# A two-layer network on one core: in the first layer's loop a key projection a step later, queries ahead of the per-token output's transposes, two side products last in their steps, and no expert sums beside the softmax

## The reference, cut to what matters

```
x = x + tanh(g_xattn[0]) * attention0(layernorm(x), ctx)     # 16 heads of 64, causal
x = x + tanh(g_ffn[0])   * mix0(layernorm(x))
x = x + tanh(g_xattn[1]) * attention1(layernorm(x), ctx)     # second layer
x = x + tanh(g_ffn[1])   * ffn1(layernorm(x))

def mix0(x):                       # every token by itself
    h = rmsnorm(x) * gamma1
    q = h @ Wq + bq                                  # 16 heads of 16
    k, v = split((h @ Wdown + bdown) @ Wup + bup)    # through 64 features
    att = softmax_over_g(q_h . k_g / 4)              # 16 x 16 for each token
    out = att @ v
    x = x + (out @ Wo + bo)
    h2 = rmsnorm(x) * gamma2
    gate = softmax(h2 @ Wg + bg)                     # 8 experts
    return x + sum_e gate[e] * (h2 @ We[e])
```

## Time and profile before

| | |
|---|---|
| median of 3 runs | 2502.51 us (2501.88 to 2504.15) |
| the profiled execution, its own time | 2502.84 us |
| its span from the first to the last instruction | 2501.0 us |
| busy: PE, DVE, ACT, POOL | 89%, 59%, 51%, 41% of the span |
| mean granted clock of TensorE | 0.961 of full speed |

### The profile page before, as it was taken

How to read it: one execution, slowest core, us unless ns; L and a number is a source line. 1 busy time by engine, 2 the same in 40 slices (tenths; PEclk the granted TensorE clock), 3 DMA queues, 4 the chain that set the end, 5 groups by cost and what they waited for, 6 DMA issues and landing times.

```text
span 2501.0 us, 47888 instructions
## 1 busy us (share of the span) xinstructions
PE 2227.4 (89%) x16000; PEld 1887.5 (75%) x16000; DVE 1480.4 (59%) x3922; ACT 1267.7 (51%) x3969; POOL 1023.1 (41%) x907
## 2 busy tenths in 40 slices
PE   5888899898888888888875799999999999999998
PEld 4667677777777777777664688888888888888888
DVE  4466666767667676676767635555555555555551
ACT  5655655556555565555633434455544444445541
POOL 1255555565555655556446213333332322333320
PEclk9999999999999999999977799999999999999999
DMA  4000000000000000000110200000000000000000
GB/s 154 8 12 14 6 17 17 17 13 4 17 17 17 13 4 17 17 17 4 39 32 13 110 16 7 13 17 17 17 17 17 17 17 16 5 13 17 17 9 9
DMA packets 26000, 51.40 MB, mean 21 GB/s; under 512 B 6160, under 2 KB 7312, under 8 KB 24784
## 3 DMA queue, kind: packets, MB, share of 16 engines
q1 hardware_dynamic: 25936, 50.57, 6.0%
HBM read 42.17 MB, written 8.39 MB: 20 GB/s over the span
## 4 chain that ended last, share of the span: by engine, by line
PE 57%; DVE 15%; ACT 8%; POOL 6%; issue 6%; DVEq 4%; POOLq 2%; DMA 0%; ACTq 0%
PE l_ffn L1714 13%; POOL l_prod L385 5%; PE l_ffn L161 4%; PE l_attn L161 4%; PE l_ffn L162 4%; PE l_ffn L163 4%; PE l_attn L1675 4%; PE l_attn L163 3%; PE l_attn L162 3%; DVEq L735 3%; PE l_side L161 3%; PE l_heads L1689 2%; POOLq L355 2%; PE l_side L163 2%; PE l_side L162 2%
## 5 line engine op out<-in xcount | busy, mean ns | idle before, releaser
L1253 POOL TENSOR_SCALAR l_probs<-l_probs,l_rinv 128x256 f32<-128x256 f32 x512 | 240.3, 484 | 479.2 <-DVE l_rinv L1492 478.3
L1376 ACT ACTIVATE l_probs<-l_score,l_negmax 128x256 f32<-128x256 f32 x512 | 239.1, 474 | 268.2 <-DVE l_negmax L1487 268.1
L385 POOL TENSOR_TENSOR l_prod<-l_att,l_kv 128x2048 f32<-128x2048 f32 x64 | 288.5, 4542 | 164.6 <-DVE l_att L672 164.6
L371 POOL TENSOR_TENSOR l_prod<-l_q,l_kv 128x2048 f32<-128x2048 f32 x64 | 291.2, 4561 | 150.7 <-DVE l_att L655 86.6
L1714 PE MATMUL l_ffn<-l_w,l_hid 128*128 128x256 f32 x1536 | 348.6, 381 | 1.0 <-ACT l_hid L1337 1.0
L1714 PEld LDWEIGHTS l_ffn<-l_w,l_hid 128*128 128x128 f32 x1536 | 286.2, 190 | 48.8 <-issue 12.7
L1499 DVE COPY l_probsT<-l_attn 128x512 f32<-128x512 f32 x240 | 164.5, 686 | 142.8 <-PE l_attn L1675 142.8
L745 DVE CUSTOM_DVE_ANT_0 l_probs<-l_score,l_mbias 128x256 f32<-128x256 f32 (+1 forms) x512 | 161.3, 352 | 144.9 <-PE l_score L947 95.8
L678 DVE TENSOR_REDUCE l_h<-l_prod 128x128 f32<-128x2048 f32 x64 | 146.3, 2286 | 107.5 <-POOL l_prod L385 107.2
L468 ACT ACTIVATE l_probs<-l_probs,l_negmax 128x256 f32<-128x256 f32 x256 | 130.8, 511 | 107.7 <-DVE l_negmax L745 106.6
L1487 DVE TENSOR_REDUCE l_negmax<-l_score 128x2 f32<-128x512 f32 x256 | 175.0, 684 | 15.0 <-PE l_score L1663 13.7
(11 more groups left out here) (261 smaller groups left out, 7177.2 us busy)
## 6 DMA issues: line engine op xcount, KB each, us to landing
l_ctxin<-in_ctx SPq DMA_DIRECT2D x32, 256.0 KB, 3.0
l_xin<-in_x SPq DMA_DIRECT2D x16, 256.0 KB, 2.6
l_x<-in_x SPq DMA_DIRECT2D x16, 256.0 KB, 2.6
x<-l_acc SPq DMA_DIRECT2D x16, 256.0 KB, 2.0
l_xin<-x SPq DMA_DIRECT2D x16, 256.0 KB, 3.1
l_x<-x SPq DMA_DIRECT2D x16, 256.0 KB, 2.6
out<-l_x SPq DMA_DIRECT2D x16, 256.0 KB, 2.0
l_hid<-in_w SPq DMA_DIRECT2D x2, 1536.0 KB, 8.2
```

The source lines that it names most:

```text
L371: nc.gpsimd.tensor_tensor(prod[:, u].rearrange("p (h g d) -> p h g d", h=half, g=H), q4[:, u * half:(u + 1) * half].unsqueeze(2).to_broadc ...
L385: nc.gpsimd.tensor_tensor(prod[:, u].rearrange("p (h d g) -> p h d g", h=half, d=HD), a4.unsqueeze(2).to_broadcast([P, half, HD, H]), v4.u ...
L1253: last = nc.gpsimd.tensor_scalar(probs[:, j % 4, t * S:(t + 1) * S], probs[:, j % 4, t * S:(t + 1) * S], rinv[:, j, t:t + 1], 1.0, ALU.mul ...
L1376: last = nc.scalar.activation(probs[:, s % 4, t * S:(t + 1) * S], ps[:, t * S:(t + 1) * S], ACT.Exp, bias=negmax[:, s, t:t + 1], accum_out ...
```

## The change

Five edits, all of them in the order of work; nothing that is computed changes. The key projection k1 of the next batch stands at step 12 instead of 11. The products of experts 4 and 6 stand at steps 13 and 16 instead of 12 and 15, and VectorE's sums of the experts 4 to 7 at 14, 15, 17 and 18 instead of 12, 14, 15 and 17. At the start of a turn TensorE projects q0 and q1 ahead of the transposes of the per-token output, ScalarE copies in the same order, and VectorE makes the variance of batch b ahead of the low part of oT. At steps 3 and 5 TensorE's side products (q at 3, up0 and the gate at 5) stand behind the transposes, values and own projections of the step instead of ahead of them. And SP's place for the store of batch B - 3 among the work of the second layer moves from 17 to 18.5.

```diff
--- before.py
+++ after.py
@@ -211,7 +211,7 @@
 
 
     own_at = {0: "k3", 1: "v1", 2: "v3", 3: "q2", 5: "q3"}
-    ahead_at = {9: "k0", 10: "xT", 11: "k1", 13: "v0", 16: "k2", 19: "v2"}
+    ahead_at = {9: "k0", 10: "xT", 12: "k1", 13: "v0", 16: "k2", 19: "v2"}
     attn_uses = ["q0", "q1"]
     for s in range(STEPS):
         attn_uses += [f"T{s - LAG_T}"] * (LAG_T <= s < H + LAG_T)
@@ -219,8 +219,8 @@
     attn = Banks(nc, left, both, "l0_attn", attn_uses + ["out"], ahead=["xT", "k0", "k1", "k2", "v0", "v2"])
 
     mix_at = {2: "hT", 3: "q", 4: "down", 5: "up0", 6: "up1"}
-    expert_at = {6: 0, 7: 1, 8: 2, 10: 3, 12: 4, 14: 5, 15: 6, 17: 7}
-    add_at = {7: 0, 8: 1, 9: 2, 10: 3, 12: 4, 14: 5, 15: 6, 17: 7}
+    expert_at = {6: 0, 7: 1, 8: 2, 10: 3, 13: 4, 14: 5, 16: 6, 17: 7}
+    add_at = {7: 0, 8: 1, 9: 2, 10: 3, 14: 4, 15: 5, 17: 6, 18: 7}
     score_at = {7: 0, 9: 1, 11: 2, 12: 3}
 
     gather_at = {15: 0, 16: 1, 18: 2, 19: 3}
@@ -312,7 +312,7 @@
             load_residual(b - 1)
             store(b - 3)
         load_residual(B - 1)
-        yield 17
+        yield 18.5
         store(B - 3)
         yield 40.6
         store(B - 2)
@@ -535,11 +535,11 @@
 
         def body(a, b, c, nxt):
             yield BEGIN
-            if c is not None:
-                high(side, "oT", c, foT[0], foT_hi)
             if a is not None:
                 project("q0", a)
                 project("q1", a)
+            if c is not None:
+                high(side, "oT", c, foT[0], foT_hi)
             for s in range(STEPS):
                 yield s - 0.6
                 if s >= 1:
@@ -821,11 +821,11 @@
 
         def body(a, b, c, nxt):
             yield BEGIN
-            if c is not None:
-                low(side, "oT", c, foT, foT_hi)
             if b is not None:
                 dve.drain()
                 variance(x1, statB, mvB, varB, varB_ready)
+            if c is not None:
+                low(side, "oT", c, foT, foT_hi)
             yield BEGIN_OUT
             if c is not None:
                 moe_residual(c)
@@ -1020,13 +1020,13 @@
 
         def body(a, b, c, nxt):
             yield BEGIN
-            if c is not None:
-                pe.wait_ge(gathered, 4 * (c + 1))
-                transpose4(side, "oT", c, o)
             if a is not None:
                 attn.emptied(pe, "xT", a)
                 project("q0", a)
                 project("q1", a)
+            if c is not None:
+                pe.wait_ge(gathered, 4 * (c + 1))
+                transpose4(side, "oT", c, o)
             yield BEGIN_OUT
             if c is not None:
                 side.emptied(pe, "oT", c)
@@ -1044,7 +1044,8 @@
                     pair_scores(a, s)
                 if a is not None and s == LAG_T:
                     head_transpose(a, 0)
-                beside_head(b, c, s)
+                if s not in (3, 5):
+                    beside_head(b, c, s)
                 if a is not None:
                     if LAG_T < s < H + LAG_T:
                         head_transpose(a, s - LAG_T)
@@ -1056,6 +1057,8 @@
                         pair_values(a, s - LAG_V0)
                     if s in own_at:
                         project(own_at[s], a)
+                if s in (3, 5):
+                    beside_head(b, c, s)
                 if nxt is not None and s in ahead_at:
                     project(ahead_at[s], nxt)
             yield STEPS
```

## The result

The changed kernel takes 2549.76 us (median of 4 runs, 2547.02 to 2552.69) against 2502.2 for the kernel before (4 runs, 2498.61 to 2504.15) beside it: a ratio of 1.0191, 95% interval 1.0174 to 1.0208. It is slower by 47.6 us; the forecast was 2505, and the range ended at 2523. The profiled execution has a span of 2549.6 us against 2501.0, and a mean granted clock of 0.951 against 0.961.

What follows compares the result with a forecast made beforehand. No engine is full; a ring closed by GpSimd's products bounds each turn. A turn changes by -0.7 us, and +0.85 for the clock: +0.15; thirteen turns +2, so 2502.84 + 2 = 2505 us, range 2488 to 2523.

Steps and rivals of the forecast that it cites:

- Both edits together: 0.9 us late: Steps 3 and 5, side products last: the scores of step 6 start 0.9 us late, bounds -0.7 and +1.5.
- The 1.1 at step 3: Step 3: q2 waits for ScalarE's copy of v3, so the scores of step 4 are 1.1 us late.
- y: The moment VectorE starts the residual sum L685; from one to the next, a turn, was 78.41 us, forecast +0.15.
- D: Start of VectorE's last score sum, y + 46.43 before; forecast at 762.7, 2.4 us earlier than 765.09.
- slower, through the new wait in step 3: Rival: the clock falls at TensorE's wait ahead of q2, up to +1.7, so +1.85 us a turn, 2527 us; chance 0.22.
- I cost that at nothing: GpSimd waits 4.01 us … a cover of 4.9: Step 5: up product and GpSimd's first product 4.1 us later, priced at nothing under a cover of 4.9 us.
- The clock behind v0: Slow clock after the new 3.6 us wait ahead of v0: between 0 and 1.7 us a turn, taken as 0.85.
- The 15.1: TensorE's time from v0 to the attention's output: 15.1 us, against 17.71 before, between ends of 14.9 and 17.7.
- The first two turns, "at 0": The first two turns, the last and the drain have only parts of the pattern: put at 0, within 3 us.
- v0 at D + 5.0: Step 13: v0 waits for ScalarE's copy of k1 and can start at D + 5.0, against D + 0.72 before.
- the gain at step 12: Step 12, key projection a step later and no expert sum: D comes 2.4 us earlier.
- the ring: The engines' chain of work that sets a turn; GpSimd's products closed it before, TensorE was to be last by a little.

Runs made afterwards that it cites:

- the filler: The changed kernel with 16 idle products of 256 columns on TensorE ahead of q2 in step 3: 2535.48 us, ratio 1.0132 against the kernel before.
- step 12 alone: The kernel before with only k1 at step 12 and the experts and their sums as in the change: 2497.8 us, ratio 0.997.

## Why the prediction was wrong

Its step **"Both edits together: 0.9 us late"** failed. That is a sum of waits with TensorE at full clock; the trace shows 4.1 us of lateness at the first score sum, in three pieces. The 1.1 at step 3 is there: the scores of step 4 at y + 13.01 where the filler keeps the clock up. The clock adds 1.5 in the change, 14.60 against 13.1. Then steps 6 to 8 add another 1.5: from the scores of step 6 to those of step 8 it takes 7.55 us (22.93 to 30.48) against 6.04 before; or, in the turns where the clock stays up there, GpSimd's lateness adds 1.25 through the stall. Of a turn's miss of 82.07 - 78.56 = 3.5 us, 3.0 lie here (D at 47.06 instead of 44.04).

The rival "slower, through the new wait in step 3" (chance 0.22, 2527 us) named the right place, but not the whole price. It had one more stretch at the lower clock, and the trace has two or one and the stall. And filling the wait gave back only 14 us, so its picture of a wait that lowers the clock just behind it is too narrow. What the runs show is that in the changed kernel the order of steps 3 and 5 costs 37 us, wherever between steps 3 and 8 the lower clock then lies.

The step **"I cost that at nothing: GpSimd waits 4.01 us … a cover of 4.9"** was wrong in kind. GpSimd's own work was indeed covered: its third product comes when VectorE's first sum is done. What I had not asked is what stands on VectorE during the time in which GpSimd is late. The normalisation L601 stood 1.0 us clear of the products' end before, and GpSimd was pushed back further than VectorE: its first product by 5.1 us (17.26 us behind y before, 22.39 in the turn from 911.86), VectorE at the scores of step 6 by 2.6. The stall costs 1.25 us in four of the full turns, and 2.7 us more than before ahead of the first y (6.69 us against 3.97).

**The clock behind v0**, at 0.85, came out larger: from v0 to the output it took 16.5 instead of 15.1, so 1.4. The half price rested on the gap of 2.45 us without a drop; in all runs here, each of the 80 full turns in which v0 waits 3.67 us or more has a stretch that starts within 2 us of v0. The 15.1 itself can be read where no stretch lies there: it is 15.25 in the change's two turns of 80.8 and 80.9, where the stretch lies ahead of v0 at y + 44.6, and 15.25 to 15.27 in three turns with steps 3 and 5 back. The first two turns, "at 0", cost 6.5: the order of steps 3 and 5 sets it off, by way of the stall: with the normalisation at step 4 the first y is at 168.86.

Right were the waits (2.15 for 2.1; 3.67 for 3.6), v0 at D + 5.0, the gain at step 12 (lateness of 4.1 becomes 0.6 at D, so 3.5; I had 0.9 and 2.4, together 3.3), from the output to the transposes 9.73 for 10.0, from there to y 3.76 for 3.6, and TensorE last in the ring. The queries' new place is in these two terms with its right size; that the old place would have been 1.7 us of a turn shorter I had not worked out. The sum of a turn with the measured terms is 47.06 + 4.99 + 16.53 + 9.73 + 3.76 = 82.07. From the first y to the fourteenth the profiled executions take 1065.06 us against 1023.08, so 42 us more, for which I had 2 (thirteen times 3.5 would be 46, but two of these turns are 80.8 and 80.9 now, and two took 80.1 and 81.3 before). With the 6.5 ahead of the first y and next to nothing behind the fourteenth this is the miss of the time (2549.76 - 2505 = 44.8 by the medians).

I also took the step 12 edit and ScalarE's order as one thing: a gain of 2.4 and a price of 4.3 at v0 that could not be had apart. They can: the copies ahead of the exponential bring v0 to D + 2.24 and turn the edit's gain from 4 us, hardly clear of the spread, into 40.

What stays open is what puts the lower clock at one place and not at another. The same wait of 2.15 us ahead of q2 is followed by a stretch at 0.50 in all turns of the change and in almost none with the normalisation at step 4, where TensorE's order is the same.

## What to carry to other kernels

When a moved piece makes an engine late by x, don't compare x with that engine's next wait alone: list what the engines beside it do in the time in which it is now busy. And where the clock has fallen once in a turn, price each new wait of TensorE at a stretch at the lower clock (here 1.5 us), as a bound of its own, and expect that gains upstream can be spent by such a stretch downstream, as the normalisation at step 4, the filler and step 12 alone show here. When an edit's gain and its price lie on two engines, look first for an order that takes the price away.

## What the runs showed of the hardware that was not expected

VectorE's two-instruction normalisation, fp32 from SBUF to SBUF with two scalars per partition, stood still until a GpSimd product already under way ended: 1.98 to 2.00 us in four turns against 0.73, and 6.69 us ahead of the first y, where each of the two ended just behind one of the two products. It shows as a longer instruction, not as a wait. The sums over GpSimd's products (L655 and L678, one fp32 input) keep their 2.26 to 2.29 beside it. The Trainium skill, SBUF — State Buffer, section Who interferes with whom, says that VectorE and GpSimd share one port pair as an exclusive lock, that a tensor_scalar can take it and a reduction never does on this chip, and that whoever comes second is blocked for the other's whole instruction; the four turns, the one ahead of the first y and the score sums agree.

A kernel with 16 idle products in each turn ran 14 us faster than the one without. And a stretch at the lower clock cost 1.5 us in one place of a turn and nothing in another: with a stretch at y + 40 v0 starts 0.5 us later and without its wait of 0.96 us for ScalarE's copy, and the attention's output starts at y + 62.82 either way.
